# One-hots of the slots laid out in pairs of choices, and a gate that follows one chunk later

## What is computed

```
x = x + gnn(layernorm(x), edge_weight, src, dst)     # 3 layers: segment_sum, l2 normalise, mean
y = layernorm(x)
gate_logits = y @ gate_w + gate_b                    # 16 experts
topk_vals, topk_idx = top_k(gate_logits, 2)
topk_w = softmax(topk_vals)
h = relu(y @ w1[e] + b1[e])                          # for both chosen experts e
expert_out = h @ w2[e] + b2[e]
x = x + layernorm(y + sum(topk_w * expert_out)) 
```

## Time and profile before

| | us |
|---|---|
| median of 3 runs | 1477.4 |
| lowest and highest | 1473.8, 1478.03 |
| the profiled execution's own time | 1478.73 |
| its span (first to last instruction) | 1477.0 |
| PE, DVE, ACT busy | 1305.6, 1076.6, 888.7 |

### The profile page before, as it was taken

The page is one execution under the profiler, slowest core; times in us unless marked ns, Lnnn a source line. Parts: engine busy times, 40 slices in busy tenths (PEclk is TensorE's granted clock), DMA queues, the critical chain, the costliest instruction groups (busy, mean ns, idle before and its releaser), DMA issues. The chain is left out here.

```text
span 1477.0 us, 31300 instructions
## 1 busy us (share of the span) xinstructions
PE 1305.6 (88%) x9556; PEld 1160.0 (79%) x9562; DVE 1076.6 (73%) x1899; ACT 888.7 (60%) x1985; POOL 235.4 (16%) x207
## 2 busy tenths in 40 slices
PE   4577777777799999999999999999969799999985
PEld 1477777777778888888888888888855699999964
DVE  8988889888777555766565765566657598888857
ACT  1788888888855554655544655545542366666653
POOL 1300000000021000000000000000000588888620
PEclk9798999999999999999999999999987699999998
DMA  5288888888886666656666656666611598989662
GB/s 190 64 210 193 194 196 200 204 198 205 215 256 207 186 178 195 186 163 186 186 176 197 183 165 185 179 195 183 182 54 37 193 310 262 287 269 279 220 202 96
DMA packets 236494, 283.03 MB, mean 192 GB/s; under 512 B 16270, under 2 KB 173046, under 8 KB 236422
## 3 DMA queue, kind: packets, MB, share of 16 engines
q1 hardware_dynamic: 228741, 261.28, 63.1%
q0 software_dynamic: 7680, 20.98, 5.1%
HBM read 194.27 MB, written 87.93 MB: 191 GB/s over the span
## 5 line engine op out<-in xcount | busy, mean ns | idle before, releaser
L869 PE MATMUL ps_rows<-h_both,a_high 128*128 (+1 forms) x1875 | 507.0, 399 | 12.3 <-ACT halves L604 5.3
L696 DVE TENSOR_TENSOR a_low<-a_raw,a_high 128x640 fp32r<-128x640 f32 x375 | 305.7, 824 | 233.4 <-ACT a_high L590 230.1
L590 ACT ACTIVATE a_high<-a_raw 128x640 fp32r<-128x640 f32 x375 | 274.4, 740 | 290.0 <-PE ps_rows L872 268.6
L869 PEld LDWEIGHTS ps_rows<-h_both,a_high 128*128 128x128 f32 x1875 | 331.1, 191 | 70.4 <-ACT halves L604 14.4
L872 PEld LDWEIGHTS ps_rows<-h_both,a_low 128*128 128x128 f32 x1875 | 276.3, 191 | 32.6
L872 PE MATMUL ps_rows<-h_both,a_low 128*128 (+1 forms) x1875 | 284.8, 283 | 0.0
L834 PE MATMUL ps_w<-lo_hot,key_w 128*120 128x160 bf16 x2736 | 236.9, 247 | 36.8 <-DVE key_w L680 36.8
L834 PEld LDWEIGHTS ps_w<-lo_hot,key_w 128*120 128x120 bf16 x2736 | 223.9, 141 | 42.8 <-ACT key_w L563 35.4
L1406 POOL DMA_INDIRECT x_t<-tokens,r_token x80 | 104.1, 1301 | 731.3 <-POOLq L891 707.5
L572 ACT ACTIVATE win<-ps_w 128x480 f32<-128x480 f32 x304 | 147.9, 570 | 53.7 <-PE ps_w L839 35.7
L680 DVE TENSOR_TENSOR key_w<-key_hot,tab_marks 128x1440 bf16<-128x1440 bf16 (+1 forms) x228 | 164.5, 776 | 0.0
(11 more groups left out here) (244 smaller groups left out, 1544.4 us busy)
## 6 DMA issues: line engine op xcount, KB each, us to landing
a_raw<-a_rows SPq DMA_DIRECT2D x375, 320.0 KB, 3.2
a_rows<-win SPq DMA_DIRECT2D x228, 240.0 KB, 3.6
w_raw<-in_L_ffn_w SPq DMA_DIRECT2D x80, 512.0 KB, 7.2
a_rows<-win SPq DMA_DIRECT2D x76, 180.0 KB
b_t<-in_L_ffn_b SPq DMA_DIRECT2D x40, 128.0 KB, 4.9
found<-results SPq DMA_DIRECT2D x6, 640.0 KB, 9.5
hf<-in_x SPq DMA_DIRECT2D x1, 3072.0 KB
x<-in_x SPq DMA_DIRECT2D x1, 3072.0 KB
```

Of the source, the lines that this page charges most:

```text
L590: a.activation(a_high[:, u, :], a_raw[:, u, :], ACT.Copy).then_inc(high_split, 1)
L696: v.tensor_tensor(a_low[:, u, :], a_raw[:, u, :], a_high[:, u, :].bitcast(F32), ALU.subtract).then_inc(low_split, 1)
L869: nc.tensor.matmul(ps[:, banks[w][r], :], a_high[:, u, r * P:(r + 1) * P], both, start=first, stop=False, skip_group_check=True)
```

## The change

It has two parts, both in `phase_route`.

The tiles of the inversion are laid out in pairs of choices: `lo_hot` becomes `[P, 25, 128, 2]`, `hi_hot` `[P, 25, 80, 2]`, `hi_no` `[P, 25, 2, 80, 2]`. Choice j is element j % 2 of pair j // 2, and what one matmul reads is 4 bytes apart. The pieces are now of 6, 6, 6 and 7 pairs (12, 12, 12 and 14 choices), the same number of elements in all. The constant tables `lo_tab` and `hi_tab` shrink to one pair (256 and 160 elements in place of 6400 and 4000), repeated by a broadcast. The instructions, their kinds, their order and their semaphores stay.

In PE's list the gate of a chunk follows three transposes behind, no longer two.

```
-            g.iota(consts.lo_tab, pattern=[[1, P], [0, K2]], base=0, channel_multiplier=0, **kw)
-            g.iota(consts.hi_tab, pattern=[[1, NS], [0, K2]], base=0, channel_multiplier=0, **kw)
-            g.iota(consts.chunk_no, pattern=[[CH, 2], [1, CH]], base=1, channel_multiplier=0, **kw)
+            g.iota(consts.lo_tab, pattern=[[1, P], [0, 2]], base=0, channel_multiplier=0, **kw)
+            g.iota(consts.hi_tab, pattern=[[1, NS], [0, 2]], base=0, channel_multiplier=0, **kw)
+            g.iota(consts.chunk_no, pattern=[[2, CH], [1, 2]], base=1, channel_multiplier=0, **kw)
...
-        PIECES = [(k, slice(a, b)) for k in range(2) for a, b in ((0, CH // 2), (CH // 2, CH))]
+        PIECES = [slice(n * CH // 4, (n + 1) * CH // 4) for n in range(4)]
...
-        lo_hot = sb("lo_hot_s", [P, P, K2], BF16)
-        hi_hot = sb("hi_hot_s", [P, NS, K2], BF16)
-        hi_no = sb("hi_no_s", [P, 2, NS, K2], BF16)
+        lo_hot = sb("lo_hot_s", [P, CH, P, 2], BF16)
+        hi_hot = sb("hi_hot_s", [P, CH, NS, 2], BF16)
+        hi_no = sb("hi_no_s", [P, CH, 2, NS, 2], BF16)
...
-                a.activation(hi_no[:, 1, :, js], hi_hot[:, :, js], ACT.Copy, scale=e_part[:]).then_inc(numbered, 1)
+                a.activation(hi_no[:, pairs, 1, :, :], hi_hot[:, pairs, :, :], ACT.Copy,
+                             scale=e_part[:]).then_inc(numbered, 1)
...
-                v.tensor_tensor(hi_hot[:, :, js], hi_tab[:, :, js], hi_b[:, js].unsqueeze(1).broadcast_to([P, NS, C]),
-                                ALU.is_equal).then_inc(hi_hot_ready, 1)
-                v.tensor_tensor(lo_hot[:, :, js], lo_tab[:, :, js], lo_b[:, js].unsqueeze(1).broadcast_to([P, P, C]),
-                                ALU.is_equal).then_inc(split_ready, 1)
+            def both(row, pairs, wide):
+                return row.rearrange("p (a q) -> p a q", q=2)[:, pairs, :].unsqueeze(2).broadcast_to(
+                    [P, pairs.stop - pairs.start, wide, 2])
...
+                v.tensor_tensor(hi_hot[:, pairs, :, :], hi_tab.unsqueeze(1).broadcast_to([P, N, NS, 2]),
+                                both(hi_b[:], pairs, NS), ALU.is_equal).then_inc(hi_hot_ready, 1)
+                v.tensor_tensor(lo_hot[:, pairs, :, :], lo_tab.unsqueeze(1).broadcast_to([P, N, P, 2]),
+                                both(lo_b[:], pairs, P), ALU.is_equal).then_inc(split_ready, 1)
...
-                v.tensor_tensor(hi_no[:, 0, :, js], hi_hot[:, :, js],
-                                chunk_no[:, k, cs].unsqueeze(1).broadcast_to([P, NS, C]),
+                v.tensor_tensor(hi_no[:, pairs, 0, :, :], hi_hot[:, pairs, :, :],
+                                chunk_no[:, pairs, :].unsqueeze(2).broadcast_to([P, N, NS, 2]),
...
-                if c >= 2:
-                    gate(c - 2)
-            gate(CH - 2)
-            gate(CH - 1)
+                if c >= 3:
+                    gate(c - 3)
+            for c in range(CH - 3, CH):
+                gate(c)
...
-                    ins = t.matmul(ps_s[:, 0:2 * NS], lo_hot[:, :, j], hi_no[:, :, :, j].rearrange("p a b -> p (a b)"),
+                    ins = t.matmul(ps_s[:, 0:2 * NS], lo_hot[:, j // 2, :, j % 2],
+                                   hi_no[:, j // 2, :, :, j % 2].rearrange("p a b -> p (a b)"),
```

More of the change, by code:

```diff
@@ L1020, in _ @@
             a.activation(ex[:], gap[:], ACT.Exp).then_inc(exp_ready, 1)
-            for n, (k, cs) in enumerate(PIECES):
+            for n, pairs in enumerate(PIECES):
                 act.wait_ge(hi_hot_ready, n + 1)
-                js = slice(k * CH + cs.start, k * CH + cs.stop)
-                a.activation(hi_no[:, 1, :, js], hi_hot[:, :, js], ACT.Copy, scale=e_part[:]).then_inc(numbered, 1)
+                a.activation(hi_no[:, pairs, 1, :, :], hi_hot[:, pairs, :, :], ACT.Copy,
+                             scale=e_part[:]).then_inc(numbered, 1)
             act.wait_ge(b1_ready, 1)
@@ L1132, in _ @@
                                  absent[:].unsqueeze(1).broadcast_to([P, 2, CH]), ALU.add))
-            for n, (k, cs) in enumerate(PIECES):
-                js = slice(k * CH + cs.start, k * CH + cs.stop)
-                C = cs.stop - cs.start
-                v.tensor_tensor(hi_hot[:, :, js], hi_tab[:, :, js], hi_b[:, js].unsqueeze(1).broadcast_to([P, NS, C]),
-                                ALU.is_equal).then_inc(hi_hot_ready, 1)
-                v.tensor_tensor(lo_hot[:, :, js], lo_tab[:, :, js], lo_b[:, js].unsqueeze(1).broadcast_to([P, P, C]),
-                                ALU.is_equal).then_inc(split_ready, 1)
+            def both(row, pairs, wide):
+                return row.rearrange("p (a q) -> p a q", q=2)[:, pairs, :].unsqueeze(2).broadcast_to(
+                    [P, pairs.stop - pairs.start, wide, 2])
+            for n, pairs in enumerate(PIECES):
+                N = pairs.stop - pairs.start
+                v.tensor_tensor(hi_hot[:, pairs, :, :], hi_tab.unsqueeze(1).broadcast_to([P, N, NS, 2]),
+                                both(hi_b[:], pairs, NS), ALU.is_equal).then_inc(hi_hot_ready, 1)
+                v.tensor_tensor(lo_hot[:, pairs, :, :], lo_tab.unsqueeze(1).broadcast_to([P, N, P, 2]),
+                                both(lo_b[:], pairs, P), ALU.is_equal).then_inc(split_ready, 1)
                 dve.wait_ge(hi_hot_ready, n + 1)
-                v.tensor_tensor(hi_no[:, 0, :, js], hi_hot[:, :, js],
-                                chunk_no[:, k, cs].unsqueeze(1).broadcast_to([P, NS, C]),
+                v.tensor_tensor(hi_no[:, pairs, 0, :, :], hi_hot[:, pairs, :, :],
+                                chunk_no[:, pairs, :].unsqueeze(2).broadcast_to([P, N, NS, 2]),
                                 ALU.mult).then_inc(split_ready, 1)
@@ L1200, in _ @@
             idle(28)
-            for n, (k, cs) in enumerate(PIECES):
+            for n, pairs in enumerate(PIECES):
                 pe.wait_ge(split_ready, 2 * (n + 1))
                 pe.wait_ge(numbered, n + 1)
-                for j in range(k * CH + cs.start, k * CH + cs.stop):
-                    ins = t.matmul(ps_s[:, 0:2 * NS], lo_hot[:, :, j], hi_no[:, :, :, j].rearrange("p a b -> p (a b)"),
+                for j in range(2 * pairs.start, 2 * pairs.stop):
+                    ins = t.matmul(ps_s[:, 0:2 * NS], lo_hot[:, j // 2, :, j % 2],
+                                   hi_no[:, j // 2, :, :, j % 2].rearrange("p a b -> p (a b)"),
                                    start=(j == 0), stop=(j == K2 - 1))
@@ L1243, in __init__ @@
         self.none = take(512, BF16)
-        self.chunk_no = take(K2, BF16).rearrange("p (k c) -> p k c", k=2)
-        self.lo_tab = take(P * K2, BF16).rearrange("p (l j) -> p l j", j=K2)
-        self.hi_tab = take(NS * K2, BF16).rearrange("p (l j) -> p l j", j=K2)
+        self.chunk_no = take(K2, BF16).rearrange("p (a q) -> p a q", q=2)
+        self.lo_tab = take(P * 2, BF16).rearrange("p (l q) -> p l q", q=2)
+        self.hi_tab = take(NS * 2, BF16).rearrange("p (l q) -> p l q", q=2)
 class Routes:
```

## The result

The changed kernel takes 1463.9 us in the median of 11 runs (1460.1 to 1471.0). The kernel before takes 1472.8 (1464.2 to 1478.0, 11 runs, the three known before the prediction among them; the other eight have a median of 1471.3). The ratio is 0.9943, 95% interval 0.9923 to 0.9963. 4.6 us of the miss of 6.6 are the starting point: three runs had given 1477.4 for a kernel whose median over eleven is 1472.8. The other 2.0 are gain: 8.9 us between the medians where 6.9 were forecast.

The account below looks back on a forecast made before the run. It took PE to bound the chunk loop, counts and inversion, DVE the stretch to the first piece. 6.3 us (inversion) plus 0.6 (gate) made 6.9, from 1477.4 to 1470.5 us; range 1465.5 to 1474.

Parts of the forecast that it names:

- What bounds the stage: Routing stage: PE ends the chunk loop, counts and inversion; DVE ends the stretch up to the first piece.
- Slot matmuls, 0.13 us at clock 0.50 and 0.077 at 1.00: Inversion on PE: each of 50 slot matmuls drops from about 0.295 us to 0.13, or 0.077 if the clock holds.
- DVE's twelve at 8.3 us: Inversion: DVE's twelve one-hot instructions take 8.3 us instead of 9.91; bounds 8.3 and 9.9.
- address or contention: Inversion: whether pieces two to four were slowed on DVE by PE's reads or by their own addresses, left untold.
- slot_part 6.4 us earlier by the inversion: End of the inversion: slot_part starts near 1147.6 instead of 1154.03; 6.3 us taken, with DVE late next.
- The rest shifts whole: After the routing stage everything moves by the gain; the second expert tile still waits for its tokens' DMA.
- The gate, 0.6 us: Chunk loop and zeros before the counts: transposes one turn earlier gain 0.6 us, bounds 0.2 and 0.8.
- A held clock: Rival, chunk loop: clock stays at 1.00, counts' matmuls come 5.1 us earlier, kernel 1466.0 us; chance 0.07.
- The starting point, 1477.4: Whole kernel: median of three earlier runs, chosen over the profiled execution's 1478.7 us as the level to subtract from.

Follow-up runs that it names:

- the series of steps: Kernel before, its 28 matmuls on zeros replaced by twelve series of 24 with operands at different element steps; 24 took 3.47 us at 8 bytes, 6.80 at 16.
- the second trace of the changed kernel: The changed kernel, nothing altered, profiled once more; 1461.1 us in that run, inversion 10.63 us, chunk loop ending at 21.17 us.
- the first table: Six traces: kernel before twice, changed kernel twice, pairs without the gate's move (ratio 0.9927), gate's move without pairs (0.9970); gives clock fall, loop end, first one-hot and inversion.
- spread loops: Kernel before with its chunk loop run twelve times after pauses of different length; mean loop end 23.15 us with the gate two behind, 21.25 with three.
- the first pair of traces: First profiled executions of the kernel before and the changed kernel; first one-hot 42.51 and 40.29 us into the routing stage.
- the parts timed alone: Against the kernel before: pair layout with the gate still two behind, 1462.8 us, ratio 0.9927; old layout with the gate three behind, 1468.3 us, 0.9970.

## Why the prediction was wrong, point by point

- **What bounds the stage** was read rightly in all four parts: PE in the loop and at the counts, DVE up to the first piece, PE in the inversion.
- **Slot matmuls, 0.13 us at clock 0.50 and 0.077 at 1.00.** The bursts of 12 in 1.78 and 1.04 us are that. That the step between elements was the cause is shown by the series of steps.
- **DVE's twelve at 8.3 us**: 8.33. The question left open there, address or contention, is answered: address.
- **slot_part 6.4 us earlier by the inversion**: 6.58. DVE, not PE, is late next, as said.
- **The rest shifts whole.** From the first gather of tokens to the end: 319.64 us before, 319.75 after. That these two agree so well is partly luck: both have the clock at 0.50 for 3.4 us some 273 us behind the first gather, and so has the second trace of the changed kernel (319.6). The three other traces of the first table don't, and take 317.0 to 317.4, whichever the kernel.
- **The gate, 0.6 us: a step that failed.** The term took the clock's instants as given, and was added up from work alone: a transpose moved into the wait at the start (0.25 us) and the stall (0.19), 0.4 at full clock and 0.8 at half. At a full clock it measured 0.62. What it left out is that the gate's place changes when the clock falls: with two behind 15 of 21 loops with a late rise had the clock down again in under 14 us, with three behind none of 20. In the spread loops 7 of 12 lose 1.3 to 3.0 us to the low clock with two behind; with three none loses more than 0.63. In the first pair of traces the term was 2.2 us. Over all with 42 zeros, six with two behind and four with three, the first one-hot comes in the mean at 42.4 and at 37.8 us: 4.6, with single traces from 37.6 to 50.1 and from 37.0 to 40.3. A held clock stood among the rivals at 0.07, as luck of the run; it was in part the change's own doing.
- **The starting point, 1477.4: the other step that failed, and by size the larger**, 4.6 of the 6.6 us. From 1472.8 the same sum gives 1465.9, within 2.0 us of the result. The three times ahead of the prediction spread over 4.2 us, eleven over 13.8, and the median of the three lay 4.6 above that of the eleven. The range had 4 us downward for the clock and the spread together. Part of the spread is ahead of the routing stage and equal for both kernels: the graph layers' last one-hot matmul began at 399.9 us in one trace of the kernel before and at 392.9 in the other.

What stays open: the parts timed alone, 0.9927 and 0.9970, add up to 15 us, the whole was timed at 8.4 and 11.0 (0.9943, 0.9925). The traces give 6.6 for the pairs and, up to the first one-hot, some 4.6 for the gate, which fits the whole; the 10.8 us of the pairs alone they don't explain. With intervals of 3 us each the sum of the parts lies at the edge of what the whole allows, and the share of each can't be read from the times. Which property of the gate's place holds the clock up is open too. Nor is it shown what makes the graph layers 7 us longer in one execution.

## What to carry to other kernels

Lay out an operand so that what one matmul streams is at most 4 bytes apart; at full clock 8 bytes cost twice and 16 bytes four times, at half clock 16 bytes cost twice, and the weights' step is free. Pairs of bf16 do that and keep DVE's runs even, and odd starts or lengths are the other thing to look for when like instructions take unlike times. A change in the order of small matmuls, or a short wait among them, may cost or save more than its length, through the clock; compare such loops only where the clock rose at the same distance before them. And when a kernel spreads over 1% from run to run, take its level from more than three runs before forecasting a time.

## What the runs showed that was not expected

- The moving columns cost 1.77 ns each at a step of 16 bytes, about that up to 50 and 2.1 at 80, and half of it at 8 bytes: 0.283 and 0.145 us for 160 columns. At 16 bytes the pace was the same at clock 1.00 and 0.50.
- A bf16 one-hot on DVE of 1536 elements took 1.50 us where its runs of 12 began at an odd element and 0.95 where they began at an even one.
- A loop of 17 us that differed from another by the place of one transpose pair, a stall of 0.19 us and some 0.2 us of wait lost up to 3 us to the clock in 12 of 30 cases and 10 us in three (the loops that ended at 32.0); the other did not lose more than 0.8.
- The same program's part behind the routing stage took 317 to 320 us on two chips and 340 to 343 on another.
